# Depthwise products of images 2 to 4 in half precision on high and low parts, with the parts split by GpSimd and the band mask read from an accumulator bank

## What is computed

```python
# block 1, for each image
xn = _layernorm_c(_gn(x), ln_w, ln_b)            # over channels, at each pixel
q  = _dwconv3x3(_conv1x1(xn, q_w), q_dw)         # 96 channels
kv = _dwconv3x3(_conv1x1(xn, kv_w), kv_dw)       # 24 + 24 channels
k, v = jnp.split(kv, 2, axis=1)
attn = softmax(einsum('bhcn,bhdn->bhcd', l2norm(q), l2norm(k)) * temperature)
x = x + _conv1x1(einsum('bhcd,bhdn->bhcn', attn, v), proj_w)
# block 2
x = x + wf @ concat([conv1x1, conv3x3, conv5x5, dilated conv3x3](_gn(x)))
```

## Time and profile before

| | us |
|---|---|
| median of three runs | 1709.13 |
| lowest and highest of the runs | 1708.07, 1710.19 |
| span of the profiled execution | 1706.1 |
| median less span | 3.0 |
| stage 2 of image 1, from the first L1428 to the last product | 106.7 |
| stage 2 of image 2 (images 3 and 4 alike) | 99.4 |

### The profile page before, as it was taken

The page is one execution under the profiler, slowest core; times in us unless marked ns, Lnnn a source line. Parts: engine busy times, 40 slices in busy tenths (PEclk is TensorE's granted clock), DMA queues, the critical chain, the costliest instruction groups (busy, mean ns, idle before and its releaser), DMA issues.

```text
span 1706.1 us, 38231 instructions
## 1 busy us (share of the span) xinstructions
PE 1652.5 (97%) x13285; PEld 1552.1 (91%) x13285; DVE 1488.7 (87%) x1964; ACT 1022.2 (60%) x1665; POOL 579.8 (34%) x398
## 2 busy tenths in 40 slices
PE   6999999999999999999999999999999999999998
PEld 6989959999999996999999996899999999599998
DVE  6788879999888859999978886999988887799997
ACT  4856576555385658545546666755446566765551
POOL 4999931222281003232247002123326400312222
PEclk9999979999999997999999999899999999799999
DMA  7012115666502201666630220366661121055553
GB/s 192 0 47 65 38 32 136 177 164 172 153 2 61 69 19 44 157 167 172 169 95 15 69 65 1 87 165 175 167 165 46 35 73 41 1 133 139 135 144 104
DMA packets 105017, 166.01 MB, mean 97 GB/s; under 512 B 40266, under 2 KB 78763, under 8 KB 104780
## 3 DMA queue, kind: packets, MB, share of 16 engines
q1 hardware_dynamic: 81772, 138.95, 32.0%
q10 hardware_dynamic: 23168, 26.04, 4.7%
HBM read 52.20 MB, written 25.17 MB: 45 GB/s over the span
## 4 chain that ended last, share of the span: by engine, by line
PE 84%; DVE 7%; issue 4%; ACT 3%; DMA 1%; DVEq 0%; SPq 0%; POOL 0%; ACTq 0%; POOLq 0%
PE ps L957 41%; PE ps L796 12%; PE ps L817 8%; PE ps L819 7%; PE ps L818 7%; PE ps L845 3%; PE ps L879 3%; PE ps L952 1%; PE ps L752 1%; ACT region L1178 1%; DVE region L1706 1%; DVE region L1676 1%; ACT region L1111 1%; DVE X L1514 1%; DVE region L1673 1%
## 5 line engine op out<-in xcount | busy, mean ns | idle before, releaser
L957 PE MATMUL ps<-region,W 128*96 128x256 f16 (+2 forms) x7140 | 800.7, 270 | 10.0 <-DMA region<-region 5.4
L957 PEld LDWEIGHTS ps<-region,W 128*96 128x96 f16 (+1 forms) x7140 | 771.3, 122 | 31.8 <-issue 14.8
L1428 DVE TENSOR_TENSOR region<-V,band 128x2322 f32<-128x2322 f32 (+2 forms) x104 | 257.8, 2488 | 59.5 <-PE ps L819 56.1
L1178 ACT ACTIVATE region<-region 96x1584 f16<-96x1584 f32 (+2 forms) x80 | 98.4, 1272 | 309.1 <-DVE region L1610 309.1
L701 POOL TENSOR_TENSOR region<-region 96x528 f32<-96x528 f32 (+1 forms) x72 | 92.0, 1282 | 445.9 <-DVE region L1676 328.4
L817 PE MATMUL ps<-region 128*128 (+1 forms) x1152 | 228.1, 280 | 10.4 <-DVE region L1428 4.5
L819 PE MATMUL ps<-region 128*128 (+1 forms) x1152 | 222.8, 275 | 0.0
L818 PE MATMUL ps<-region 128*128 (+1 forms) x1152 | 222.2, 274 | 0.0
L1706 DVE SCALAR_TENSOR_TENSOR region<-ps,small,region 96x768 f32<-96x768 f32 (+1 forms) x220 | 203.7, 988 | 12.1 <-PE ps L957 10.4
L796 PE MATMUL ps<-proj,region 96*128 96x240 f32 x1024 | 209.3, 367 | 0.6 <-DVE region L1402 0.6
L796 PEld LDWEIGHTS ps<-proj,region 96*128 96x128 f32 x1024 | 194.8, 191 | 14.1 <-DVE region L1402 1.0
(11 more groups left out here) (234 smaller groups left out, 2199.8 us busy)
## 6 DMA issues: line engine op xcount, KB each, us to landing
region<-region SPq DMA_DIRECT2D x104, 247.5 KB, 3.9
region<-in_x_dram SPq DMA_DIRECT2D x128, 192.0 KB, 2.3
out_dram<-region SPq DMA_DIRECT2D x40, 576.0 KB, 4.2
region<-region ACTq DMA_DIRECT2D x72, 247.5 KB, 2.4
X<-in_x_dram SPq DMA_DIRECT2D x30, 576.0 KB, 6.2
region<-region SPq DMA_DIRECT2D x32, 247.4 KB, 4.9
X<-in_x_dram SPq DMA_DIRECT2D x19, 384.0 KB, 10.6
region<-region SPq DMA_DIRECT2D x24, 185.6 KB, 3.7
```

What stands on the lines that cost most here:

```text
L957: last = mm(o, w, src, start=k == 0, stop=k == len(steps) - 1, skip_group_check=split and ck > 0)
L1178: act.activation(dst[0:C, a:e, x:z], src, ACT.Copy, scale=1.0 if whole else col(SA)).then_inc(s_h, 1)
L1428: v.tensor_tensor(T[:, i, 3 * c:3 * c + m].rearrange("p m (i j) -> p m i j", j=3), taps.broadcast_to([P, m, BW // 3, 3]), mask.broadcast_t ...
```

## The change

For images 2 to 4 each channel's values and each tap are split into two float16 numbers, high and low, and a product becomes three float16 products: high matrix by high values, high by low, and low by high. A chunk then has 54 products instead of 18. GpSimd makes the value parts chunk by chunk (`query_split`): a copy to float16 and a subtraction, 768 elements each, into two buffers for the high parts and in place for the low ones. The taps are split once, on VectorE after the bands of image 1. `bands` then makes two float16 sets with two instructions of 2376 elements each (18 matrices of 132 columns). TensorE waits for one more semaphore, `s_qsp`.

For all images the mask is float16 and is read from PSUM bank 0, where VectorE puts it once an image near the end of stage 1. Image 1 keeps its float32 products. The taps lie in `V` in another order (the three diagonals next to each other). The scale that was folded into the taps of q and k is now shared between the projection and all taps, and is taken out where the sums are evicted; the low parts' instruction gets a factor for that. Buffers of stage 1 and 3 move; one of six value strips is dropped, so the strip of the last rows is placed later in ScalarE's order.

```diff
-        V = sb("V", [P, 3, 3 * CO])
-        band = sb("band", [P, BW])
+        Vf = sb("V", [P, 9 * CO])
+        V = Vf[:].rearrange("p (m j) -> p m j", j=3)
+        V16 = Vf[:].bitcast(f16).rearrange("p (n k e) -> p n k e", n=DK, k=2)
+        band = sb("band", [P, BW16], f16)
...
+        T16 = work[:, 1536:1536 + 2 * DM * BW16].bitcast(f16).rearrange("p (i k m x) -> p i k m x", i=2, k=2, m=DM)
+        QH = span(EXTRA_AT, DC * H).bitcast(f16).rearrange("p (i c h) -> p i c h", i=2, c=DC)
+        QL = span(Q_AT, WORK).bitcast(f16).rearrange("p (n e) -> p n e", n=DK)[:, :, 0:DC * H].rearrange("p n (c h) -> p n c h", c=DC)
...
-        KEPT = VPAIRS - EARLY
+        KEPT = 5
...
-            turning.done(pool.tensor_scalar(V[:, :, 0:3 * QK], V[:, :, 0:3 * QK], col(QKS, P), None, ALU.mult))
+            turning.done(pool.tensor_scalar(Vf[:], Vf[:], col(TAPGAIN, P), None, ALU.mult))
...
+                def query_split(k2, i, parts):
+                    n = k2 * 2 + i
+                    done = (b - 1) * DK + n
+                    pool.wait_ge(s_dw, b * DK + n - 1 + START)
+                    for at, (c, channels) in enumerate(parts):
+                        rows = Q[:, bass.ds(n * DC + c, channels), :]
+                        high = QH[:, i, c:c + channels]
+                        step = len(PARTS_OF_T) // len(parts)
+                        pool.tensor_copy(high, rows).then_inc(s_qh, step)
+                        pool.wait_ge(s_qh, done * len(PARTS_OF_T) + (at + 1) * step + START)
+                        pool.tensor_tensor(QL[:, bass.ds(n, 1), c:c + channels].rearrange("p o c h -> p (o c) h"), rows, high,
+                                           ALU.subtract).then_inc(s_qsp, step)
...
+                                if b:
+                                    pe.wait_ge(s_qsp, (n - DK) * len(PARTS_OF_T) + ready + START)
...
+                            if b:
+                                high = QH[:, i, c]
+                                low = QL[:, bass.ds(k2 * 2 + i, 1), c].rearrange("p o h -> p (o h)")
+                                for tap, to, x in ((1, 0, 0), (0, 1, 0), (2, 0, 1)):
+                                    n_ = H - to - x
+                                    for part, src in ((0, high), (0, low), (1, high)):
+                                        last = mm(o[:, to:to + n_], T16[:, i, part, 3 * c + tap, 0:W], src[:, x:x + n_],
+                                                  start=(tap, part) == (1, 0) and src is high, stop=(tap, part) == (2, 1))
+                                continue
...
-                for k in range(KEPT, VPAIRS):
+                for k in range(KEPT, VPAIRS - 1):
                     values(k)
...
                 act.activation(col(TMAX), epsc[0:C, 0:1], ACT.Exp)
+                values(VPAIRS - 1)
...
+                    if i == 1:
+                        mask = ps[:, 0, 0:BW16 // 2]
+                        dve.wait_ge(s_pq, (b + 1) * AT - AD + 1 + START)
+                        v.tensor_scalar(mask.bitcast(i32), band[:].bitcast(i32), 0x3C003C00, None, ALU.bitwise_and).then_inc(s_mask, 1)
+                mask16 = mask.bitcast(f16)
...
+                        if b:
+                            wide = mask16.rearrange("p (i j) -> p i j", j=3).unsqueeze(1).broadcast_to([P, m, BW16 // 3, 3])
+                            for part in range(2):
+                                taps = V16[:, bass.ds(k2 * 2 + i, 1), 1 - part, 9 * c:9 * c + 3 * m] \
+                                    .rearrange("p o (m j) -> p (o m) j", j=3).unsqueeze(2)
+                                step = v.tensor_tensor(T16[:, i, part, 3 * c:3 * c + m].rearrange("p m (i j) -> p m i j", j=3),
+                                                       taps.broadcast_to([P, m, BW16 // 3, 3]), wide, ALU.mult)
+                            step.then_inc(s_T, len(PARTS_OF_T) // len(parts))
+                            continue
...
+                if b < 1:
+                    whole_taps = Vf[:].rearrange("p (n e) -> p n e", n=DK)
+                    dve.wait_ge(s_T, DK * len(PARTS_OF_T) + START)
+                    v.tensor_copy(VH, whole_taps).then_inc(s_vsp, 1)
+                    dve.wait_ge(s_vsp, 1)
+                    v.tensor_tensor(V16[:, :, 0], whole_taps, VH, ALU.subtract).then_inc(s_vsp, 1)
+                    dve.wait_ge(s_vsp, 2)
+                    v.tensor_copy(V16[:, :, 1], VH).then_inc(s_vsp, 1)
```

More of the change, by code:

```diff
@@ L61, in build_program @@
     WTOP = 1024.0
+    QTOP, TAPTOP = 16384.0, 2048.0
+    HLSCALE = 2.0 ** -12
     OR = 3
@@ L146, in build_program @@
         ps = ctx.enter_context(nc.psum_tensor("ps", [P, 8, BANK], f32))
-        pq = region[:, 0:2 * AR * CO].rearrange("p (i r c) -> p i r c", i=2, r=AR)
-        y1 = work[0:C, 0:AD * BANK].rearrange("p (i n) -> p i n", i=AD)
-        sq = [t.rearrange("p (r c) -> p r c", r=AR) for t in (region[:, 1152:1152 + AR * C], work[:, 2048:2048 + AR * C])]
-        vr, sd, rr = (work[:, a:a + AD * AR].rearrange("p (i r) -> p i r", i=AD) for a in (2432, 2448, 2464))
+        span = lambda at, n: region[:, at:at + n]
+        chunk_of = lambda i: ps[:, 4 + 2 * i:6 + 2 * i, :].rearrange("p k n -> p (k n)")[:, 0:DC * H]
+        pq = [span(at, AR * CO).rearrange("p (r c) -> p r c", r=AR) for at in (0, EXTRA_AT)]
+        SQ_AT = EXTRA_AT + AR * CO
+        Y1_AT = SQ_AT + AR * C
+        sq = [span(at, AR * C).rearrange("p (r c) -> p r c", r=AR) for at in (SQ_AT, Y1_AT + AD * BANK)]
+        y1 = region[0:C, Y1_AT:Y1_AT + AD * BANK].rearrange("p (i n) -> p i n", i=AD)
+        vr, sd, rr = (span(at, AD * AR).rearrange("p (i r) -> p i r", i=AD) for at in (576, 592, 608))
+        assert AR * CO <= 576 and 624 <= Q_AT
         stage = [work[0:C, j * BANK:(j + 1) * BANK] for j in range(3)]
@@ L165, in build_program @@
         EARLY = 2
-        KEPT = VPAIRS - EARLY
+        KEPT = 5
         vs = [t.rearrange("p (r c) -> p r c", r=VR) for t in
-              [region[:, GROUPS_QK * SLOT + k * VR * VP:GROUPS_QK * SLOT + (k + 1) * VR * VP] for k in range(3)] +
+              [span(GROUPS_QK * SLOT, VR * VP), span(EXTRA_AT, VR * VP)] +
               [work[:, AT * P + k * VR * VP:AT * P + (k + 1) * VR * VP] for k in range(3)]]
@@ L237, in build_program @@
         sqfold = Qf[0:C, 10400:10400 + 5 * 5 * C].rearrange("p (y n) -> p y n", y=5)
-        tapsum = Qf[:, 10200:10200 + QK]
+        tapsum = Qf[:, 10200:10200 + CO]
+        wideband = work[:, 4096:4096 + BW16]
         def col(i, n=C):
@@ L570, in _ @@
                     turn = small[:, at:at + 1]
-                    product = turned if d else V[:, j, :]
+                    product = turned if d else V[:, :, j]
                     turning.done(pool.tensor_scalar(product, rawdw[:, :, d], turn, None, ALU.mult))
@@ L650, in _ @@
                     split_weights()
+                def query_split(k2, i, parts):
[10 more added lines that the diff above has]
+                                           ALU.subtract).then_inc(s_qsp, step)
+                if b > 0:
+                    pool.wait_ge(s_q, (b + 1) * (AT - 1) + START)
+                    pool.wait_ge(s_pq, (b + 1) * AT + START)
+                    query_split(0, 0, PARTS_OF_T)
+                    query_split(0, 1, ((0, DC),))
+                    with pool.Fori(1, DK // 2) as k2:
+                        for i in range(2):
+                            query_split(k2, i, ((0, DC),))
                 def first_planes():
@@ L986, in summed @@
                 piece = X[:, SUMMED[j] * LR * W:(SUMMED[j] + 1) * LR * W]
-                unused = region[0:C, 0:LR * W]
+                unused = work[0:C, 0:LR * W]
                 act.wait_ge(s_first[SUMMED[j]], 16)
```

90 lines of the change are left out of this document (54 added, 36 removed).

## The result

| | before | changed |
|---|---|---|
| median, us (four runs each) | 1708.99 | 1718.53 |
| lowest and highest, us | 1708.07, 1710.19 | 1716.98, 1719.48 |
| span of the profiled execution, us | 1706.1 | 1716.1 |

The ratio is 1.0053, 95% interval 1.0039 to 1.0066: the change makes the kernel slower by 9.5 us, where 31 us less were forecast. The time lies inside the range on record, 1655 to 1746, which had been widened to take in rival 2.

What follows compares the result with a forecast made beforehand. TensorE was taken to set the pace in images 2 to 4, with VectorE and GpSimd in each other's way in image 1. 1706.1 - 7.3 - 28.2 + 4.0 = 1674.6, with 3.0 around it 1677.6 us; range 1655 to 1746.

Steps and rivals of the forecast that it cites:

- rival 2: Stage 2, images 2 to 4: TensorE has a floor of 0.086 us per product, kernel 1746 us; chance 0.11.
- By bytes it would be two elements per cycle: VectorE's float16 band instructions, images 2 to 4: 2376 elements in 1.39 us each, bounds 0.78 and 2.63.
- the turn of the sign: Band instructions on VectorE: from 1.78 us each, 4.27 per chunk, the change would make the kernel slower.
- Image 1: Stage 2 of image 1: with the mask in PSUM bands fall from 3.01 to 2.58 us, stage to 99.4, -7.3 us.
- TensorE, 0.058 us per product: Images 2 to 4: float16 products of 128 columns follow at 0.058 us, 3.13 us per chunk of 54.
- The weight load: TensorE: a load of 128 float16 columns takes 137 ns, about 55 for the columns, and keeps up with the products.
- The loop: Images 2 to 4: 7.45 us from chunk n to n+2, 3.73 per chunk, TensorE waiting behind low parts; -28.2 us in all.
- GpSimd's part: Value split per chunk in images 2 to 4: 3.1 us beside VectorE's 3.95, costs nothing, with cover of 0.8 us.
- rival 3: GpSimd's subtraction stays at 3.85 us rather than 1.64, chunk 4.43 us, kernel 1720 us; chance 0.04.
- What it adds: Extra work outside the gains: taps' scaling and setup +1.0, mask +0.8, value strip before the exponential +2.2, sum +4.0 us.
- The 3.0 us around the span: Time added to the forecast span of 1674.6 us to give the kernel's forecast of 1677.6 us.
- Rival 1: VectorE's float16 bands in images 2 to 4 run at one element per cycle, 5.97 us per chunk, kernel 1839; chance 0.13.

Runs made afterwards that it cites:

- Experiment 1: Changed kernel with GpSimd repeating each chunk's taps twice side by side, so that band instructions of images 2 to 4 read rows of six: 1676.38 us, ratio 0.9803.
- experiment 3: Kernel before with one part of the change, the float16 mask read from PSUM in all images: 1702.44 us, ratio 0.9954.
- experiment 8: Kernel of experiment 6 without the low band matrices' instruction, TensorE multiplying the high ones instead (output not the reference's): 1638.35 us, one execution.
- experiment 6: Changed kernel with rows of six, proj and cbias scaling off VectorE's chain, taps' scaling out of the way and one repeat moved: 1672.48 us, ratio 0.9790.
- experiments 7 and 10: 7: changed kernel's band instruction probed, rows of 6 or 132 with mask in SBUF: 1.99, 1.97 us. 10: experiment 6 with mask in SBUF: 1782.95 us.

## Why the prediction was wrong

**The failed step: "By bytes it would be two elements per cycle, 2376 x 0.52 + 0.16 = 1.39 us; I take this."** It is 1.80. With two float16 inputs, one in PSUM, two elements per cycle are real (1.385 us with taps in a row of 132), but not for taps in rows of three from SBUF: each row of 6 bytes touches two 4-byte words, and takes two cycles for its three elements. I had counted bytes, not rows. The form of the operand was in the diff (`j=3`, broadcast over 44), but in float32 it costs nothing, since by the same count a row of three elements is three words and three cycles, so no row of before could show it. The prediction had put the turn of the sign at 1.78 us per instruction and 4.27 per chunk; measured were 1.80 and 4.28, just past the turn, and so the forecast gain of 9.4 us per image became a loss of 4. Experiment 1 changes the rows, with GpSimd's repeat for it, and gives 1676.4. The turn itself was put too high. It was counted over some twenty chunks of a stage, but all 24 have their bands: at 4.28 per chunk the stage is 103.4, and at the turn it had to be 100.5 (99.4 and a third of 7.3 - 4.0). At 0.48 us of stage for each 0.01 us of a band instruction the turn lay near 1.74, an estimate from these two lengths.

That the time lies inside the range is luck: the upper end stood for slower products on TensorE, and those did not come.

What the prediction weighed from two pages of the Trainium skill is off for this form. VectorE: DVE Perf Modes, "The perf-mode tier table", has 1x for any operand in PSUM, where 2376 elements took 1188 + 142 cycles. The Vector Engine (DVE) Microarchitecture Reference, "Performance modes — why throughput varies by op and dtype", lets pairs of a two-source instruction span two rows of odd length and finds no difference from 4-byte alignment. By that all these forms would take the 1188 + 142 cycles, 1.385 us; 1.49 for rows of eleven, 1.80 for rows of three and 1.795 for six from an odd element don't fit it.

**Image 1**: right in mechanism and size, 6.5 us for 7.3; experiment 3 shows that the mask's place alone does it. The bands fell to 2.57 us as forecast. The 0.8 us that are missing are the stage's own 100.2 against image 2's 99.4, a length near that of image 4 before; why, no run shows.

**TensorE, 0.058 us per product**: right, 0.0572 in experiment 8. The weight load was not: 0.46 ns per column are 59 ns for 128 columns, not 55, and by 59 the load would have been level with the product; the whole load took 98 ns and not 137. Rival 2, a floor of 0.086 that turns the sign from 0.076 on, is refuted, and the 0.081 weighed beside it is not borne out.

**The loop**: 3.73 us per chunk was worked out for 1.39 us bands; with these bands, in experiments 1 and 6, it is 3.6, and the stage 88.5 where 90.0 were forecast. In experiment 6 the chunk of 547.22 and the next but one, of 554.44, are 7.22 us apart, not 7.45: the two signals take about 0.38 and 0.25, not 0.43 and 0.38. The kernels of both experiments even have the repeat in them. (The 0.223 per product of the kernel before is its pace inside a chunk; 4.09/18 is 0.227.)

**GpSimd's part and rival 3**: right, its subtraction took 1.65 us beside bands with one SBUF input. Its cover is not there at a stage's start: TensorE waited 2.7 us for the split in experiment 1. What rival 3 feared happens with the mask in SBUF, in experiments 7 and 10. The Trainium skill says the same in GPSIMD Engine Reference, "Specifications": contention with VectorE instructions that have two SBUF inputs.

**What it adds**: forecast 4.0; the spans show 4.6 in the setup and 0.9 behind the stages, 5.5. The setup was mis-sized: +1.0 was taken, mainly for GpSimd's queue. VectorE's chain was overlooked, with 1.21 us for `proj` and 0.91 for `cbias` beside a busy GpSimd, and 1.49 instead of 1.25 for the wider sum of the taps. The +0.6 of GpSimd's scaling came true: VectorE's wait for it is 2.44 us, not 1.78. About 1 us of the 4.6 is a later first product (12.82 against 11.75), which differs between traces anyhow (11.75 to 13.06). The value strip and the mask were put too high, 3.0 against 0.9: the strip is 0.84 us and started at 638.24, while VectorE was still at the softmax, so that the exponential was 0.3 us later, not 0.56; the mask's copy takes 0.22 and in experiment 3 moves nothing that can be seen.

**The 3.0 us around the span**: in every execution of these runs the time is only 1.7 to 2.0 us over the span (1717.89 and 1716.1 for the changed kernel). The other 1.2 is that the profiled execution of the kernel before was faster than its median; as the forecast is a difference from that median, nothing hangs on it.

Rival 1 named the right instruction, but no size in between: it had 1 element per cycle or 2, and the truth was 1.5.

## What to carry to other kernels

Before pricing a 16-bit instruction of VectorE with two inputs by elements or bytes, look at how each operand is read: here, with one input in PSUM, a short row from SBUF that is read again and again cost a cycle for each 4-byte word it touches. So make rows even and begin them at an even element, and let an idle engine repeat a row if need be (216 elements copied by GpSimd bought back 15 us per image). An operand in PSUM instead of SBUF frees both VectorE and GpSimd from each other, and can be had alone: here it gave 7.6 us on the kernel before. When a balance hangs on one unit price, state where its sign turns, and look for what could lie between the two bounds.

## What the runs showed of the hardware

- A two-input float16 instruction with one input in PSUM runs at two elements per cycle (1.385 us for 2376) where the repeated row is even and begins at an even element; otherwise it takes a cycle for each 4-byte word that the rows of taps touch, as the table has it. Rows with gaps (1.50) are not explained.
- With both inputs in SBUF beside a working GpSimd the same instruction took 1.97 to 2.54 us on average, and GpSimd's cast up to 1.99 instead of 0.82 and its subtraction up to 3.14 instead of 1.65.
- Float16 weight loads of 128 columns took 98 ns on average here, less than the 122 of the loads of 96 columns in the earlier trace rows, from whose slope I had 137. Why, no run shows.
- TensorE's float16 products of 128 columns follow at 0.0572 us with a weight load each.
